# Mixture-of-experts stage: the down product turned round in three fp16 products, with tokens as columns

## The reference

```python
weights, idx = _gate(x, w_gate)
combine = (jax.nn.one_hot(idx, E, dtype=x.dtype) * weights[..., None]).sum(1)
g = jax.nn.silu(jnp.einsum('th,efh->tef', x, w1_e))
u = jnp.einsum('th,efh->tef', x, w3_e)
routed = jnp.einsum('tef,ehf,te->th', g * u, w2_e, combine)
shared = _swiglu(x, w1_s, w3_s, w2_s)
return (routed + shared).reshape(shape)
```

## Time and profile before

| | us |
|---|---|
| three timed runs, median (lowest to highest) | 2321.24 (2319.95 to 2324.96) |
| the profiled execution | 2319.1 |
| its span in the trace | 2317.3 |
| TensorE busy | 2037.8 (88%) |
| VectorE / ScalarE / GpSimd busy | 1625.4 / 1308.5 / 1000.9 |
| granted clock of TensorE, mean | 0.947 of 2.4 GHz |
| experts, first matmul to the last addition | 1098.2 to 1296.1 |

### The profile page before, as it was taken

One profiled execution on the slowest core, in us unless ns is written; L12 is line 12 of the kernel. 1 busy time (PEld: TensorE's weight loads), 2 busy tenths in 40 slices (PEclk: granted clock), 3 DMA queues, 4 the chain that ended last, 5 costly groups with the idle time before them and its releaser, 6 DMA issues. The chain is left out here.

```text
span 2317.3 us, 56731 instructions
## 1 busy us (share of the span) xinstructions
PE 2037.8 (88%) x18115; PEld 1061.5 (46%) x18115; DVE 1625.4 (70%) x3414; ACT 1308.5 (56%) x2072; POOL 1000.9 (43%) x867
## 2 busy tenths in 40 slices
PE   5569999999999999983999759999999999998566
PEld 3434444444444444453555323444444444443345
DVE  4778888888888888866544676666666666664696
ACT  2236666666666666642222346777778787877121
POOL 1133222322322332421000226787878787877454
PEclk9779999999999999976999988999999999999787
DMA  5522212221222221100000271111111111100000
GB/s 134 149 62 56 53 48 53 54 50 50 55 52 48 54 54 49 37 11 1 1 0 0 92 232 36 42 31 38 34 34 37 31 38 31 41 14 1 1 14 23
DMA packets 126924, 106.60 MB, mean 46 GB/s; under 512 B 39636, under 2 KB 102724, under 8 KB 126860
## 3 DMA queue, kind: packets, MB, share of 16 engines
q1 hardware_dynamic: 124640, 103.37, 16.8%
q10 hardware_dynamic: 2220, 2.45, 0.4%
HBM read 75.81 MB, written 29.53 MB: 45 GB/s over the span
## 5 line engine op out<-in xcount | busy, mean ns | idle before, releaser
L1049 DVE TENSOR_REDUCE b_mx<-psum 128x1 f32<-128x512 f32 x1024 | 663.9, 686 | 143.3 <-PE psum L868 81.0
L1033 ACT ACTIVATE b_prob<-psum 128x1024 f32<-128x1024 f32 x512 | 523.9, 1023 | 317.9 <-PE psum L900 317.8
L1736 POOL TENSOR_TENSOR f_plo<-f_prob,f_phi 128x512 f16<-128x512 f32 x512 | 586.5, 1156 | 164.4 <-ACT f_phi L1861 140.1
L1879 DVE TENSOR_REDUCE f_mx<-psum 128x1 f32<-128x512 f32 x512 | 328.7, 683 | 169.1 <-PE psum L1756 168.1
L1860 ACT ACTIVATE f_prob<-psum 128x512 f32<-128x512 f32 x512 | 307.3, 600 | 150.8 <-PE psum L1767 149.7
L948 PE MATMUL psum<-b_prob,b_v 128*32 128x256 f32 x4096 | 327.4, 391 | 1.6 <-ACT b_prob L1033 0.5
L1861 ACT ACTIVATE f_phi<-psum 128x512 f16<-128x512 f32 x512 | 306.0, 598 | 0.0
L804 POOL COPY b_v<-v 128x64 f32 x64 | 15.1, 236 | 596.1 <-PE psum L948 595.7
L900 PE MATMUL psum<-b_diag,b_toep 128*128 128x79 f16 (+1 forms) x4224 | 266.6, 208 | 0.0
L807 POOL TENSOR_TENSOR b_diag<-flip,grev 128x1024 f16<-128x1024 f16 x128 | 239.6, 1892 | 0.0
L900 PEld LDWEIGHTS psum<-b_diag,b_toep 128*128 128x128 f16 x4224 | 235.2, 99 | 9.0 <-issue 2.6
(11 more groups left out here) (301 smaller groups left out, 3432.4 us busy)
## 6 DMA issues: line engine op xcount, KB each, us to landing
d_qk<-e_qk SPq DMA_DIRECT2D x64, 256.0 KB, 2.6
b_toep<-d_line SPq DMA_DIRECT2D x128, 64.0 KB
f_qa<-d_qk SPq DMA_DIRECT2D x64, 128.0 KB, 2.9
f_ka<-d_qk SPq DMA_DIRECT2D x64, 128.0 KB, 2.9
b_q<-d_q SPq DMA_DIRECT2D x128, 54.0 KB
d_k<-a_qk SPq DMA_DIRECT2D x48, 128.0 KB, 2.3
b_toep<-d_line SPq DMA_DIRECT2D x128, 32.0 KB
b_q<-b_m SPq DMA_DIRECT2D x256, 1.0 KB
```

What stands on the lines that cost most here:

```text
L1033: nc.scalar.activation(prob[:, t % 4, :].rearrange("p (a n) -> p a n", a=2), ps[:, EXP + 2 * (t % 2):EXP + 2 * (t % 2) + 2, :], ACT.Exp).t ...
L1049: nc.vector.tensor_reduce(mx[:, b, t, half:half + 1], ps[:, bank, :], AX.X, ALU.max).then_inc(s.max_read, 1)
L1736: nc.gpsimd.tensor_tensor(plo[:, t % 4, at], prob[:, t % 4, at], phi[:, t % 4, at], ALU.subtract).then_inc(s.plo_ready, 1)
L1879: nc.vector.tensor_reduce(mx[:, b, t, half:half + 1], ps[:, MAX + half, :], AX.X, ALU.max).then_inc(s.max_read, 1)
```

## The change

1. `down` has the down weights as the stationary operand and the hidden values as the moving one, with 512 tokens as columns. It is made of three fp16 matmuls: high weights by high hidden, low weights by high hidden, high weights by low hidden. For that ScalarE makes the high part of d_hid (`high`, into d_h16), and GpSimd subtracts it for the low part.
2. The sum now has features as rows. ScalarE copies it from PSUM to SBUF once a chunk (`copy_out`), TensorE turns it with four fp32 transposes into the same bank (`turn_out`), and VectorE adds that to x. These steps of chunk n-1 stand inside chunk n, behind its units 2, 4 and 5.
3. TensorE makes `up` two units ahead of `down` (LAG = 2).
4. `g.combT` and the constant `g.expert` have 128 rows, of which rows 32 to 127 are zero; GpSimd clears those of combT with two memsets during routing.
5. The split on GpSimd takes in the nine down tiles (35 tiles in one pair of instructions; before, 18 and 8 in two pairs).
6. VectorE quantises the last layer's weights in five pieces of 224 columns, and the last layer's hidden values share the memory of `g.w16`.

```diff
-    expert = np.zeros((2, NE, NE // 2, P), np.float16)
+    expert = np.zeros((P // NE, NE, NE // 2, P), np.float16)
     for e in range(NE):
-        expert[:, e, e // 2, (e % 2) * FE:(e % 2 + 1) * FE] = 1
+        expert[:2, e, e // 2, (e % 2) * FE:(e % 2 + 1) * FE] = 1
...
-        "c_expert": expert.reshape(2 * NE, NE // 2, P),
+        "c_expert": expert.reshape(P, NE // 2, P),
...
-SPLIT = [*range(W_1, W_2), *range(W_Q1, W_V1)]
+SPLIT = [*range(W_1, W_V1)]
...
-        WH = (UPS + FI) // 2
+        PIECES = 5
+        WH = (UPS + FI) // PIECES
         wt = quant_scratch(ctx, nc, "bw", WH)
...
-                for i, (x, y) in enumerate(((W_1, W_2), (W_Q1, W_V1))):
-                    at = slice(IN_16[x], IN_16[x] + y - x)
-                    nc.gpsimd.tensor_copy(g.w16[:, 0, at, :], g.wT[:, x:y, :]).then_inc(s.pool_set, 1)
-                    pool.wait_ge(s.pool_set, 4 + 2 * i)
-                    nc.gpsimd.tensor_tensor(g.w16[:, 1, at, :], g.wT[:, x:y, :], g.w16[:, 0, at, :], ALU.subtract).then_inc(s.pool_set, 1)
-                    pool.wait_ge(s.pool_set, 5 + 2 * i)
+                nc.gpsimd.tensor_copy(g.w16[:, 0, :, :], g.wT[:, W_1:W_V1, :]).then_inc(s.pool_set, 1)
+                pool.wait_ge(s.pool_set, 4)
+                nc.gpsimd.tensor_tensor(g.w16[:, 1, :, :], g.wT[:, W_1:W_V1, :], g.w16[:, 0, :, :], ALU.subtract).then_inc(s.pool_set, 1)
+                pool.wait_ge(s.pool_set, 5)
...
                 items(dve, item_steps)
                 dve.wait_ge(w_loaded, 16 * (2 * len(FC) + 1))
                 link = chain(dve, w_chain)
-                for half in range(2):
-                    w = g.wgud[:, half * WH:(half + 1) * WH]
+                for piece in range(PIECES):
+                    w = g.wgud[:, piece * WH:(piece + 1) * WH]
                     link(quantise(nc.vector, w, w, WH // QB, wt, link))
                 divide_o(H0 - 1, B - 1)
...
+            @block.gpsimd
+            def _(pool):
+
+                nc.gpsimd.memset(g.combT[2 * NE:4 * NE, :].bitcast(F32), 0.0)
+                nc.gpsimd.memset(g.combT[4 * NE:P, :].bitcast(F32), 0.0)
...
-                    nc.scalar.copy(g.combT[:, c * CHUNK:(c + 1) * CHUNK], ps[0:2 * NE, c, :])
...
+        RING, LAG = 3, 2
+        COPY_STEP, TURN_STEP, ADD_STEP = 2, 4, 5
...
-        hid = sb("d_hid", [P, 3, CHUNK])
+        hid = sb("d_hid", [P, RING, CHUNK])
+        h16 = sb("d_h16", [P, RING, 2, CHUNK], F16)
+        outT = sb("d_outT", [P, 2, CHUNK])
...
+        def chunks(eng, body):
+
+            body(0, 0, True, False)
+            with eng.Fori(0, NC // 2 - 1) as i:
+                body(2 * i + 1, 1, False, False)
+                body(2 * i + 2, 0, False, False)
+            body(NC - 1, 1, False, True)
 
         with nc.Block() as block:
 
             @block.tensor
             def _(pe):
-                credit(pe, s.gate_psum, s.up_psum, s.down_psum, s.out_psum)
+                credit(pe, s.gate_psum, s.up_psum, s.down_psum, s.out_turned)
...
                 def down(n, u, f):
+
                     j = FT * n + f
-                    pe.wait_ge(s.hid_ready, done(j))
+                    w = [g.w16[:, part, IN_16[W_2 + f], :] for part in range(2)]
+                    out = ps[:, OUT + u, :]
                     if f == 0:
                         pe.wait_ge(s.out_added, done(n - 2))
+                    pe.wait_ge(s.hi_ready, done(j))
+                    nc.tensor.matmul(out, w[0], h16[:, f % RING, 0, :], start=f == 0, stop=False)
+                    nc.tensor.matmul(out, w[1], h16[:, f % RING, 0, :], start=False, stop=False)
+                    pe.wait_ge(s.lo_ready, done(j))
+                    nc.tensor.matmul(out, w[0], h16[:, f % RING, 1, :], start=False, stop=f == FT - 1).then_inc(s.down_psum, 1)
+
+                def turn_out(n, u):
+                    pe.wait_ge(s.out_copied, done(n))
                     for k in range(CT):
-                        last = nc.tensor.matmul(ps[:, OUT + u, k * P:(k + 1) * P], hid[:, f % 3, k * P:(k + 1) * P], g.wT[:, W_2 + f, :],
-                                                start=(f, k) == (0, 0), stop=f == FT - 1, skip_group_check=True)
-                    last.then_inc(s.down_psum, 1)
-
-                up(0, 0, 0)
-
-                def chunk(n, u, last):
+                        last = nc.tensor.transpose(ps[:, OUT + u, k * P:(k + 1) * P], outT[:, u, k * P:(k + 1) * P], g.ident[:, :])
+                    last.then_inc(s.out_turned, 1)
+
+                for f in range(LAG):
+                    up(0, 0, f)
+
+                def chunk(n, u, first, last):
+                    for f in range(FT):
+                        if f + LAG < FT:
+                            up(n, u, f + LAG)
+                        elif not last:
+                            up(n + 1, 1 - u, f + LAG - FT)
+                        down(n, u, f)
+                        if f == TURN_STEP and not first:
+                            turn_out(n - 1, 1 - u)
+
+                chunks(pe, chunk)
+                turn_out(NC - 1, 1)
+
+            @block.scalar
+            def _(act):
+                credit(act, s.silu_ready, s.hi_ready, s.out_copied)
+
+                def silu(n, u, f):
+                    j, r = FT * n + f, (FT * u + f) % 2
+                    act.wait_ge(s.gate_psum, done(j))
+                    act.wait_ge(s.prod_ready, done(j - 2))
+                    nc.scalar.activation(act_g[:, r, :], ps[:, GATE + r, :], ACT.Silu).then_inc(s.silu_ready, 1)
+
+                def high(n, f):
+                    j = FT * n + f
+                    act.wait_ge(s.hid_ready, done(j))
+                    act.wait_ge(s.down_psum, done(j - RING))
+                    nc.scalar.copy(h16[:, f % RING, 0, :], hid[:, f % RING, :]).then_inc(s.hi_ready, 1)
+
+                def copy_out(n, u):
+                    act.wait_ge(s.down_psum, done(FT * n + FT - 1))
+                    act.wait_ge(s.out_turned, done(n - 2))
+                    nc.scalar.copy(outT[:, u, :], ps[:, OUT + u, :]).then_inc(s.out_copied, 1)
+
+                silu(0, 0, 0)
+
+                def chunk(n, u, first, last):
                     for f in range(FT):
                         if f + 1 < FT:
-                            up(n, u, f + 1)
+                            silu(n, u, f + 1)
                         elif not last:
-                            up(n + 1, 1 - u, 0)
-                        down(n, u, f)
-
-                steps(pe, chunk)
-
-            @block.scalar
-            def _(act):
-                credit(act, s.silu_ready)
-
-                def chunk(n, u, last):
+                            silu(n + 1, 1 - u, 0)
+                        high(n, f)
+                        if f == COPY_STEP and not first:
+                            copy_out(n - 1, 1 - u)
+
+                chunks(act, chunk)
+                copy_out(NC - 1, 1)
+
+            @block.gpsimd
+            def _(pool):
+                credit(pool, s.lo_ready)
+
+                def chunk(n, u, first, last):
                     for f in range(FT):
-                        j, r = FT * n + f, (FT * u + f) % 2
-                        act.wait_ge(s.gate_psum, done(j))
-                        act.wait_ge(s.prod_ready, done(j - 2))
-                        nc.scalar.activation(act_g[:, r, :], ps[:, GATE + r, :], ACT.Silu).then_inc(s.silu_ready, 1)
-
-                steps(act, chunk)
+                        j = FT * n + f
+                        pool.wait_ge(s.hi_ready, done(j))
+                        nc.gpsimd.tensor_tensor(h16[:, f % RING, 1, :], hid[:, f % RING, :], h16[:, f % RING, 0, :], ALU.subtract).then_inc(s.lo_ready, 1)
+
+                chunks(pool, chunk)
 
             @block.vector
             def _(dve):
                 credit(dve, s.prod_ready, s.hid_ready, s.out_added)
 
                 def add_out(n, u):
-                    dve.wait_ge(s.down_psum, done(FT * n + FT - 1))
+                    dve.wait_ge(s.out_turned, done(n))
                     t = bass.ds(n * CT, CT)
                     nc.vector.tensor_tensor(g.x[:, t, :], g.x[:, t, :], ps[:, OUT + u, :].rearrange("p (t e) -> p t e", t=CT), ALU.add).then_inc(s.out_added, 1)
 
-                def chunk(n, u, last):
+                def chunk(n, u, first, last):
                     for f in range(FT):
                         j, r = FT * n + f, (FT * u + f) % 2
                         dve.wait_ge(s.silu_ready, done(j))
...
                         if f < FT - 1:
                             nc.vector.tensor_tensor(prod[:, r, :], act_g[:, r, :], ps[:, UP + r, :], ALU.mult).then_inc(s.prod_ready, 1)
                             dve.wait_ge(s.prod_ready, done(j))
-                            dve.wait_ge(s.down_psum, done(j - 3))
-                            nc.vector.tensor_tensor(hid[:, f % 3, :], prod[:, r, :], ps[:, COMB + r, :], ALU.mult).then_inc(s.hid_ready, 1)
+                            dve.wait_ge(s.lo_ready, done(j - RING))
```

(43 more changed lines are left out.)

## The result

| | before | after |
|---|---|---|
| runs of the first comparison, median (lowest to highest), us | 2323.1 (2319.95 to 2326.06), 4 runs | 2308.9 (2306.81 to 2315.67), 4 runs |
| ratio to before [95%] | | 0.994 [0.992, 0.997] |
| the profiled execution / its span, us | 2319.1 / 2317.3 | 2315.67 / 2313.9 |
| experts, first matmul to the end of the last addition, us | 197.9 | 163.0 |
| attention 0, first to last exponential, us | 859.6 | 877.8 |

The kernel became faster, by 14.2 us instead of the 29 in the forecast's sum, and 2308.9 lies above the whole range of 2283 to 2304. The stage that was changed took the time that was forecast. The two attentions became longer, though their loops were not touched.

A forecast was written before the change was run, and what follows sets the result against it. It took TensorE, busy 191.2 of the experts' 197.9 us, as the bound. Terms: 2319.1 - 34.8 (experts) + 5.1 (quantisation) + 0.7 (c_expert) = 2290.1 us for the profiled execution; forecast 2291, range 2283 to 2304.

The forecast's parts named there:

- the down product: Experts: each unit swaps eight fp32 passes (1.00 or 0.89 us) for three fp16 matmuls, 0.65 us; stage 163.1 against 197.9.
- the padding: Routing product in the experts: with 128 rows instead of 32, its two wide steps fall from 0.31 to 0.216 us.
- Turning the sum: Experts: four fp32 transposes per chunk cost TensorE 0.50 us, 4.0 in all; copy and addition lie beside TensorE's work.
- The lag and the chain: Experts: two units of lag cover the chain to the low part with 0.8 us spare; the old 6.0 us of waits go.
- Rival (b): Experts: the chain is longer than two units, paid in every unit; with 1.1 instead of 0.8, 2313 us; chance 0.07.
- (c): Experts: GpSimd's subtraction and VectorE's multiplications exclude each other; a unit of 2.8 us, kernel 2335 us; chance 0.04.
- (d): Experts: ScalarE reloads its table between Silu and copy, 2.6 us a unit; kernel 2400 us; chance 0.02.
- Quantisation: Tail of attention 0: five pieces add 27 linked VectorE instructions, 5.1 us that nothing covers; bounds 4.3 to 5.7.
- c_expert: Loading of constants: this one grows by 192 KB, costing 0.7 us, from 0 to 1.0.
- The clock behind attention 0: Phase behind attention 0, mean clock 0.61: 5 us more TensorE idling ahead of it, taken as 0, plus or minus 3 us.
- The split on GpSimd: End of attention 0: 1152 more columns take 3.3 us, covered because its last instruction began 38 us before the phase ends.
- The base: Start of the sum: profiled execution at 2319.1 us; the median of the runs is 2.1 above it.

The follow-up runs named there:

- The two comparisons: Both kernels timed, then again without edits: 2308.9 us against 2323.1 at first, then 2311.23 us against 2332.72, ratio 0.990.
- early_pieces: Changed kernel, quantising once inside the last attention item, ScalarE's loop moved 40 instructions, GpSimd's cast and subtraction in seven pieces, last subtraction in two: 2281.8 us, ratio 0.980.

## Why the prediction was wrong, point by point

- **What bounds the kernel, the down product, the padding**: right. 0.216 a step, a stage of 163.0 against 163.1 forecast, padding 11.5 against 12.8. That the stage's time fits to 0.1 us is in part luck. Beside the 153.8 of the fp16 matmuls I had 4.0 for transposes, 1.4 for the start, 1.0 for table loads and 2.9 for the end. From TensorE's starts in the trace of after I read 3.5, 0.2 and none, and 2.3 for a wait once a chunk that the prediction put at nothing; 3.2 are left for the end.
- **Turning the sum**: four transposes took 0.44 (1274.91 to 1275.35) against 0.50.
- **The lag and the chain**: right but for that wait. "The sum was turned a unit before" was to make VectorE's addition free, but VectorE waited 1.9 us for the turned sum, and the low part behind it came 0.4 late, in six chunks. `high` took 0.61 from SBUF. Rival (b) is out as a wait in every unit, and so is (c) as it was put: 0.69 beside GpSimd. Of the table loads, one was seen (L1476) where I had paid 1.0 for repeated ones, and (d) is out.
- **Quantisation**: right, +5.1; TensorE's next phase began 5.3 later behind the last exponential.
- **c_expert**: attention 0 began 1.7 later in this profile, 0.7 forecast; but the starts spread from 146.6 to 149.2 in the profiles of changed kernels and from 145.9 to 148.1 in those of the kernel before, so neither number is shown.
- **The clock behind attention 0**: from the start of phase_output0 to routing it was 45.6 us instead of 48.4, at 0.72 instead of 0.61: inside the plus or minus 3.
- **The split on GpSimd, "3.3 us, and that cover is ample"**: wrong. I had asked only whether GpSimd would be done in time. The question was also who shares something with it while it runs. VectorE's cast had 1.34 us in the profile of before, against 0.17 at other items, and I had not looked. The term stood at nothing, and the last item became 4.2 us longer.
- **Attention 1**: no term at all stood for it. Added code moved a loop, and the loop then loaded instructions in each pass: 6.4 us.
- **The base**: I took the profiled execution for the typical one. It had no stall; most executions seem to have some, and 2319.1 was near the fastest that this kernel does.

The sum, from profile to profile: 2315.67 - 2319.1 = -3.4. Two stalls are in it, which make attention 0 longer by 18.2 - 4.2 = 14.0. Without them it is -17.4. (The 14.0 is what is left of the stage, not a measurement of its own; two stalls at 6 to 8 us are 12 to 16.) The forecast change was -29.0; with the two missing terms and a start 1.0 later it is -29.0 + 6.4 + 4.2 + 1.0 = -17.4. The rest, above all -2.8 in phase_output0 and +2.4 behind attention 1 (whose cause I did not look for), adds up to nothing, and that is luck. The two comparisons gave -14.2 and -21.5, on both sides of it. None of my rivals named what happened: all four were about the stage of the change.

So the forecast failed at the cover of GpSimd's split, put at nothing and worth 4.2 us, at attention 1, for which no term stood and which took 6.4, and at a base without stalls. The first two are 10.6 of the 14.8 us that are missing from the change of the medians; how much of the rest is stalls, the runs without a profile don't show.

What stays open: why TensorE's loop in attention 0 is loaded again in some passes and not in others, with a stall at the start of each such pass. The code of the loop lies at the same place in both compiled programs, and both have stalls; early_pieces shows none in its profile, but one of its six runs took 2320.71. Whether the two comparisons differ by the count of stalls alone can't be said, since runs without a profile don't show theirs.

## What to carry to other kernels

When a change makes an instruction of GpSimd longer, look in the trace for the VectorE instructions beside it that are longer than their like elsewhere: here they told beforehand what the longer one would hold up, however well it was covered itself. A loop that isn't touched can still cost more when code ahead of it grows, so compare the stages that nobody changed, and the DMA view's instruction loads, before explaining a total; idle instructions ahead of the loop test it both ways. Before a profile serves as the base of a sum, see whether it is a lucky one: count its stalls, and hold its time against the spread of the runs. And when a stage takes just the time that was forecast, add up its terms one by one before calling them right.

## What the hardware showed that I had not expected

- 88 instructions that do nothing, ahead of a loop of 289 on ScalarE, made attention 1 longer by 7.6 us (726.4 to 734.0); 40 more ahead of the loop of the changed kernel made it 6.1 shorter (732.8 to 726.7).
- In 860 to 900 us of one loop TensorE stops 0 to 6 times, each time for 3.6 to 4.9 us at the start of a pass, and nine instruction loads of 16 KB follow in that pass. Such a pass takes 59.4 to 61.4 us instead of 54.0, part of it by the lower clock behind the stop.
- A VectorE cast of 128 x 8 elements takes from 0.17 to 3.16 us by what GpSimd does, and 1.8 us more of it went with a last item that was 4.2 longer.
